# A causal attention layer: ScalarE's copy of the weighed sums, one block of keys earlier in its queue

## The chip, the cores and the metric

The kernel runs on one core of a Trainium2 chip. The metric is the time of one execution on the device, in microseconds (us), as the median of several runs.

## The reference, cut to what matters

The program is a stack of eight layers on x of 4 x 1024 x 128, each added to its input: a state space layer, an expert layer, a landmark attention, an expert layer, a causal attention, an expert layer, an attention with memory, an expert layer. Only the causal attention (16 heads of 8 dimensions, 1024 positions, 4 batches) is touched:

```python
q = q * cos + rotate_half(q) * sin
k = k * cos + rotate_half(k) * sin
bias = rel_bias_table[bucket].transpose(2, 0, 1)
att = (jnp.einsum('bhid,bhjd->bhij', q, k) + bias[None]) * (1.0 / math.sqrt(D))
att = jnp.where(causal[None, None], att, -jnp.inf)
att = jax.nn.softmax(att, axis=-1)
y = jnp.einsum('bhij,bhjd->bhid', att, v)
return y.transpose(0, 2, 1, 3).reshape(B, T, C) @ Wp + bp
```

## The kernel before

`causal_layer` works through 16 units: u = 4 * batch + group, a group being G4 = 4 of the 16 heads. In a unit the queries come in two sets of 512 (q4 = 0 and 1), and each set meets tiles of 128 keys (kt): 4 tiles for the first set, 8 for the second, so `blocks` lists 12 pairs (q4, kt), bi = 0 to 11. Blocks 0 and 4 are the first of a new set of queries.

For each block and head j, TensorE multiplies keys by queries into one of three PSUM banks (4 to 6, `tile_bank`; line 1603). Where keys and queries lie near each other a bias is added, for even j by three matmuls on TensorE (line 1607), for odd j by VectorE (line 1742). ScalarE takes the exponential into `pt` (line 1503). TensorE multiplies the values by `pt` and gathers the weighed sums of the four heads over the key tiles in bank 7 (`products`, line 1625). When a set of queries is through, ScalarE copies bank 7 into `ysb` (`copy_y`, line 1511), and the next set may then overwrite it: the first products of a set (kt == 0) wait for the semaphore `y_copied`, the copy waits for `pv_done`, which counts products. TensorE later transposes `ysb` (`gather_y`, line 1632), and VectorE divides by the sum of weights.

Between the scores TensorE makes, for the next unit, products of queries and keys (`top`, line 1581), of which VectorE takes maxima (lines 1728 and 1729). These, and the projections (line 1545), transposes and outputs of other batches, take turns in two slots of banks 0 to 3; `claim` waits until VectorE or ScalarE has emptied a slot. Projections stand in blocks 4 and 6 of the first two units of a batch, for the batch after it; the values' product (line 1559, moved out by ScalarE at line 1486) stands in block 0 of the third.

The order of all this is written out by hand in `walk`. Each engine runs `walk` with its own functions, and leaves out the steps it has none for, so `walk` is the order of each queue. In an iteration (u, bi) it gives: the scores of heads 0 and 1, a maximum's product, the scores of heads 2 and 3, another, then `products`, then `copy_y` where it is due, then the rest. `products(u, bi)` is always one block behind: it works on block bi - 1, and for bi = 0 on block 11 of the unit before. On ScalarE `scores` are the exponentials. So on ScalarE `copy_y(u, bi)` stands behind the four exponentials of block bi, and on TensorE `products(u, bi)` behind the four scores of block bi.

Of the kernel before, what the change touches and what calls it, by code (L numbers as in the profile page):

```python
# [1183 lines left out]
def causal_layer(nc, g, wq, bq, wk, bk, wv, bv, wp, bp, table, wq_sw, bq_sw, wk_sw, bk_sw, rope, onehot):  # L1184
# [8 lines left out]
    G4 = 4  # L1193
    NG = H // G4
    U = BATCH * NG
# [4 lines left out]
    blocks = [(q4, kt) for q4 in range(2) for kt in range(4 * q4 + 4)]  # L1200
    NB = len(blocks)
    NS = NB * G4
# [14 lines left out]
    def walk(turn_x=idle, project=idle, split=idle, values=idle, turn_bias=idle, stack=idle, top=idle, join=idle, lower=idle,  # L1217
             scores=idle, products=idle, copy_y=idle, gather_y=idle, turn_y=idle, out=idle):
        n = 1
        turn_x(0, n)  # L1220
        n += 1
        for side in range(2):
            for h in range(2):
                project(0, side, h, n)
                n += 1
            for part in range(4):
                split(0, side, part)
        for u in range(3):
            stack(u)
        values(0, n)  # L1230
        n += 1
        for gr in range(NG):
            turn_bias(gr, n)
            n += 1

        def maxima(v, first, count):
            nonlocal n
            u, vb = v // NB + 1, v % NB
            base = sum(QUOTA[(i - LAG) % NB] for i in range(vb))
            for t in range(base + first, base + first + count):  # L1240
                if u < U:
                    top(u, t, n)
                    n += 1
                if u < U and t == ROWS - 1:
                    join(u)

        for t in range(ROWS):
            top(0, t, n)
            n += 1
        join(0)  # L1250
        lower(0, n)
        n += 1
        for v in range(LAG):
            maxima(v, 0, QUOTA[(v - LAG) % NB])
        for u in range(U):
            b, gr = u // NG, u % NG
            for bi in range(NB):
                v = u * NB + bi + LAG
                if bi == 0 and 1 <= u < U - 2:
                    stack(u + 2)  # L1260
                scores(u, bi, 0)
                maxima(v, 0, 1)
                scores(u, bi, 2)
                maxima(v, 1, 1)
                if u or bi:
                    products(u, bi)
                if blocks[bi][1] == 1 and (u or bi > 1):
                    copy_y(u, bi)
                if bi == NB - LAG and u + 1 < U:
                    lower(u + 1, n)  # L1270
                    n += 1
                maxima(v, 2, QUOTA[bi] - 2)
                if bi == 2 and u:
                    gather_y(u - 1, n)
                    n += 1
                if bi == 3 and gr == 0 and b:
                    turn_y(b - 1, n)
                    n += 1
                if bi == 5 and gr == 0 and b:
                    out(b - 1, n)  # L1280
                    n += 1
                if b + 1 < BATCH:
                    if gr == 0 and bi == 1:
                        turn_x(b + 1, n)
                        n += 1
                    for side in range(2):
                        if gr == side and bi in (4, 6):
                            project(b + 1, side, bi // 2 - 2, n)
                            n += 1
                        if gr == side and bi in (7, 8, 9, 10):  # L1290
                            split(b + 1, side, bi - 7)
                    if gr == 2 and bi == 0:
                        values(b + 1, n)
                        n += 1
        products(U, 0)
        copy_y(U, 1)
        gather_y(U - 1, n)
        turn_y(BATCH - 1, n + 1)
        out(BATCH - 1, n + 2)

    with ExitStack() as ctx:
# [53 lines left out]
        st_ready, bias_added, p_ready, pv_done = (s.sem(n) for n in ("st_ready", "bias_added", "p_ready", "pv_done"))  # L1355
        y_copied, yy_ready, oT_ready, x_added = (s.sem(n) for n in ("y_copied", "yy_ready", "oT_ready", "x_added"))

        def slot(n):
            return ps[:, 2 * (n % 2):2 * (n % 2) + 2, :]

        def slot_row(n):
            return slot(n).rearrange("p a b -> p (a b)")
# [7 lines left out]
        def by_vector(bi, j):  # L1370
            return bi in near and j % 2 == 1
# [4 lines left out]
        with nc.Block() as block:  # L1376
# [77 lines left out]
            @block.scalar  # L1454
            def _(act):
                nc.scalar.activation(norm_std[:], g.MV[:, :, 1], ACT.Sqrt, bias=g.eps[:, 0:1]).then_inc(std_ready, 1)

                def turn_bias(gr, n):
                    heads = slice(gr * G4 // 2, gr * G4 // 2 + G4 // 2)
                    turned = slot_row(n).rearrange("p (h r w) -> p r h w", r=2, w=W2)  # L1460
                    act.wait_ge(slot_filled, n + 1)
                    nc.scalar.activation(bias_kp[:, 0, heads], turned[:, 0], ACT.Copy).then_inc(bias_copied, 1)
                    nc.scalar.activation(bias_kd[:, heads], turned[:, 1], ACT.Copy).then_inc(bias_copied, 1)
                    act.wait_ge(bias_rest1, gr + 1)
                    nc.scalar.activation(bias_kp[:, 1, heads], bias_rest[:, gr], ACT.Copy).then_inc(bias2, 1)

                def turn_x(b, n):
                    act.wait_ge(slot_filled, n + 1)
                    nc.scalar.activation(xt[:], slot_row(n), ACT.Copy).then_inc(xt_ready, 1)
                    act.wait_ge(xt_ready, b + 1)  # L1470
                    act.sem_inc(slot_free[n % 2], 1)

                def split(b, side, part):
                    k = b * 2 + side
                    if part == 0:
                        act.wait_ge(full_ready, k * 2 + 2)
                        if k:
                            act.wait_ge(pieces_stored[1 - side], (k + 1) // 2 * NP * 16)
                        nc.scalar.activation(piece[:, 0, :], full[:], ACT.Copy).then_inc(piece1, 1)
                    if part == 2:  # L1480
                        act.wait_ge(rest1, k + 1)
                        nc.scalar.activation(piece[:, 1, :], full[:], ACT.Copy).then_inc(piece2, 1)

                def values(b, n):
                    act.wait_ge(slot_filled, n + 1)
                    nc.scalar.activation(vp[:, b % 2, :, :, 0:D], slot(n).rearrange("p a (t h d) -> p (a t) h d", t=CT, d=D), ACT.Copy).then_inc(vp_ready, 1)
                    act.wait_ge(vp_ready, b + 1)
                    act.sem_inc(slot_free[n % 2], 1)

                def scores(u, bi, j0):  # L1490
                    lo, mid, hi = span(*blocks[bi])
                    c0 = blocks[bi][0] * CHUNK
                    for j in range(j0, j0 + 2):
                        i = u * NS + bi * G4 + j
                        if by_vector(bi, j):
                            act.wait_ge(bias_added, added(u, bi, j))
                        else:
                            act.wait_ge(st_ready, i + 1)
                        if i >= 8:
                            act.wait_ge(pv_done, i - 7)  # L1500
                        if i == 0:
                            act.wait_ge(bias_split, NG)
                        nc.scalar.activation(pt[:, i % 8, lo - c0:hi - c0], ps[:, tile_bank(i), lo - c0:hi - c0], ACT.Exp, scale=SCALE).then_inc(p_ready, 1)  # L1503

                def copy_y(u, bi):
                    q4 = 1 if bi == 1 else 0
                    k = 2 * u + (bi > 1) - 1
                    act.wait_ge(pv_done, u * NS + (0 if bi == 1 else 4 * G4))
                    if k >= 2:
                        act.wait_ge(yy_ready, k // 2)  # L1510
                    nc.scalar.activation(ysb[:, k % 2, :], ps[:, 7, :], ACT.Copy).then_inc(y_copied, 1)  # L1511

                def turn_y(b, n):
                    act.wait_ge(slot_filled, n + 1)
                    nc.scalar.activation(oT, slot_row(n), ACT.Copy).then_inc(oT_ready, 1)
                    act.wait_ge(oT_ready, b + 1)
                    act.sem_inc(slot_free[n % 2], 1)

                walk(turn_x=turn_x, split=split, values=values, turn_bias=turn_bias, scores=scores, copy_y=copy_y, turn_y=turn_y)

            @block.tensor
# [882 lines left out]
```

## Time and profile before

| | us |
|---|---|
| median of 3 runs | 2743.92 |
| lowest, highest | 2735.3, 2744.12 |
| profiled execution | 2740.05 |
| its span | 2738.3 |
| TensorE busy, matmuls | 2201.8 (80%) |
| VectorE busy | 1766.9 (65%) |
| ScalarE busy | 1464.6 (53%) |
| causal layer, about | 850 to 1634 of the span |

The span runs from the first to the last instruction of the profiled execution. In the rows PE is TensorE's matmuls and PEld its weight loads, which overlap them; DVE is VectorE, ACT ScalarE, POOL GpSimd. An fp32 product is recorded as two matmuls, so four heads' products are "x8". The time in brackets at a row's end is how long the engine had been idle before it, with the instruction whose end released it.

### The profile page before, as it was taken

What the parts mean: (1) busy time and instruction counts of PE and PEld (TensorE: products, weight loads), DVE (VectorE), ACT (ScalarE), POOL (GpSimd) and SP (SyncE); (2) the same over time, 40 slices, a digit from 0 to 9 for tenths busy, and PEclk for the clock granted to TensorE, in tenths of its full rate; (3) what the DMA queues carried; (4) which work ended last, traced back from release to release, by engine and by line L of the source; (5) the groups of instructions that cost most, each with busy time, mean ns of one, the idle gap of its engine ahead of it and who ended that gap; (6) DMA issues with size and microseconds to landing.
All of it is one profiled execution on the core that took longest, in us unless ns stands there. A gap on an engine that the chain in (4) does not pass through costs nothing. (4 is left out here: it accounts for less than half of the span.)

```text
span 2738.3 us, 79111 instructions
## 1 busy us (share of the span) xinstructions
PE 2201.8 (80%) x30448; PEld 1559.9 (57%) x30448; DVE 1766.9 (65%) x5714; ACT 1464.6 (53%) x3712; POOL 1058.0 (39%) x1032
## 2 busy tenths in 40 slices
PE   6499948599946888888888877948989898889686
PEld 3188835288832333333333335836777777777486
DVE  6723348623347776776867734359999999999622
ACT  5455544355532455454554545537766676666353
POOL 2156644056651101000000003637766676666164
PEclk7599979599976998998989888979999999999798
DMA  4011120011135111110110001121111111111012
GB/s 127 34 41 43 43 76 1 33 41 43 43 107 152 51 32 34 34 44 19 42 36 22 16 6 48 42 84 54 51 50 52 52 50 52 52 50 50 36 41 89
DMA packets 76023, 134.94 MB, mean 49 GB/s; under 512 B 17225, under 2 KB 32264, under 8 KB 73224
## 3 DMA queue, kind: packets, MB, share of 16 engines
q1 hardware_dynamic: 62080, 102.07, 12.1%
q0 software_dynamic: 13568, 27.81, 3.5%
q8 instruction: 250, 4.10, 0.6%
q14 instruction: 117, 0.96, 0.1%
q10 hardware_dynamic: 8, 0.00, 0.0%
HBM read 65.19 MB, written 32.79 MB: 36 GB/s over the span
## 5 line engine op out<-in xcount | busy, mean ns | idle before, releaser
L1503 ACT ACTIVATE ca_pt<-ca_ps 128x512 f32<-128x512 f32 (+3 forms) x768 | 340.8, 491 | 375.1 <-PE ca_ps L1607 171.7
L733 PE MATMUL ffn_ps<-ffn_xst,ffn_up_w 128*128 128x128 f32 x3392 | 421.2, 278 | 0.2 <-issue 0.2
L733 PEld LDWEIGHTS ffn_ps<-ffn_xst,ffn_up_w 128*128 128x128 f32 x3392 | 403.3, 195 | 1.2 <-issue 1.2
L856 DVE TENSOR_TENSOR ffn_hid<-ffn_sg,ffn_ps 128x512 f32<-128x512 f32 x212 | 145.9, 688 | 333.9 <-PE ffn_ps L733 242.8
L580 POOL DMA_INDIRECT ffn_y<-ffn_ys,ffn_result_at x212 | 208.9, 985 | 222.0 <-DVE ffn_ys L862 191.3
L575 POOL DMA_INDIRECT ffn_xs<-ffn_x,ffn_token_at x212 | 205.2, 968 | 230.8 <-DVE ffn_token_at L839 133.4
L1603 PE MATMUL ca_ps<-ca_stacks 75*128 75x512 bf16 (+3 forms) x768 | 252.5, 352 | 18.0 <-ACT ca_pt L1503 12.6
L1728 DVE TENSOR_REDUCE ca_m_far<-ca_ps 128x1 f32<-128x128 f32 (+5 forms) x384 | 236.5, 616 | 46.4 <-PE ca_ps L1581 44.8
L1581 PE MATMUL ca_ps<-ca_stacks 72*128 72x512 bf16 (+3 forms) x768 | 229.1, 365 | 41.3 <-DVE ca_m_near L1729 28.7
L543 POOL MEMSET ffn_gate_wide<- 128x32 f32 x4 | 0.5, 126 | 580.0 <-POOLq L42 580.0
L1936 POOL TENSOR_TENSOR im_pt_e<-im_pt,im_own 128x512 f32<-128x512 f32 x128 | 162.7, 1271 | 156.6 <-DVE im_pt L2195 154.5
L1625 PE MATMUL ca_ps<-ca_pt,ca_vp 128*9 128x512 f32 (+3 forms) x1536 | 181.0, 545 | 42.5 <-ACT ca_ysb L1511 42.5
L1729 DVE CUSTOM_DVE_ANT_0 ca_spill<-ca_ps,ca_bias_q 128x256 f32<-128x256 f32 (+1 forms) x512 | 200.7, 397 | 18.0 <-PE ca_ps L1581 18.0
L642 ACT ACTIVATE ffn_sg<-ffn_ps 128x512 f32<-128x512 f32 x212 | 126.4, 596 | 131.9 <-PE ffn_ps L733 123.9
L1943 POOL TENSOR_TENSOR im_rope_qk<-im_t,im_mates 128x512 f32<-128x512 f32 x128 | 171.9, 1343 | 52.1 <-DMA im_mates<-im_t 49.6
L741 PE MATMUL ffn_ps<-w_w,ffn_hid 128*128 x1136 | 156.1, 280 | 34.6 <-DVE ffn_ys L862 34.5
L1949 POOL TENSOR_TENSOR im_el<-im_ee,im_rr 128x512 f32<-128x512 f32 x128 | 163.3, 1276 | 34.7 <-ACT im_ee L1987 33.4
L1742 DVE TENSOR_TENSOR ca_ps<-ca_ps,ca_bias_kd 128x256 f32<-128x256 f32 (+1 forms) x288 | 109.7, 382 | 94.4 <-PE ca_ps L1603 90.7
L1581 PEld LDWEIGHTS ca_ps<-ca_stacks 72*128 72x128 bf16 x768 | 67.8, 103 | 177.1 <-DVE ca_m_near L1729 98.1
L741 PEld LDWEIGHTS ffn_ps<-w_w,ffn_hid 128*128 128x128 f32 x1136 | 137.8, 191 | 49.1 <-issue 49.1
L862 DVE COPY ffn_ys<-ffn_ps 128x128 f32<-128x128 f32 x212 | 61.8, 292 | 152.4 <-remote 81.0
L1603 PEld LDWEIGHTS ca_ps<-ca_stacks 75*128 75x128 bf16 x768 | 78.2, 102 | 142.0 <-ACT ca_pt L1503 73.2
(336 smaller groups left out, 4926.3 us busy)
## 6 DMA issues: line engine op xcount, KB each, us to landing
im_mates<-im_t SPq DMA_DIRECT2D x256, 128.0 KB
ffn_got<-ffn_y SPq DMA_DIRECT2D x48, 256.0 KB, 5.7
ca_stacks<-scratch_q_piece SPq DMA_DIRECT2D x16, 576.0 KB
ca_stacks<-scratch_k_piece SPq DMA_DIRECT2D x48, 192.0 KB
ffn_x<-ffn_xn SPq DMA_DIRECT2D x32, 256.0 KB, 2.0
w_w<-in_L_ffn_experts_w_dram SPq DMA_DIRECT2D x2, 2048.0 KB, 11.8
ffn_xs<-ffn_x,ffn_token_at POOLq DMA_INDIRECT x212
ffn_y<-ffn_ys,ffn_result_at POOLq DMA_INDIRECT x212
```

The lines of the kernel that those rows point to most:

```text
L575: nc.gpsimd.indirect_dma_start(out=xs[:, n % XS, :], out_offset=None, in_=xn_rows[:, :], in_offset=bass.IndirectOffsetOnAxis(ap=token_at[: ...
L580: nc.gpsimd.indirect_dma_start(out=y_rows[:, :], out_offset=bass.IndirectOffsetOnAxis(ap=result_at[:, n:n + 1], axis=0), in_=ys[:, n % YS, ...
L733: last = nc.tensor.matmul(ps[:, bank, j * P:j * P + P], up_w[:, n % WS, first + j * P:first + j * P + P], xst[:, n % 2, :], start=True, st ...
L741: last = nc.tensor.matmul(ps[:, 5, 0:P], hid[:, n % 2, j * P:j * P + P], down(e, j), start=(j == 0), stop=(j == IB - 1))
L1503: nc.scalar.activation(pt[:, i % 8, lo - c0:hi - c0], ps[:, tile_bank(i), lo - c0:hi - c0], ACT.Exp, scale=SCALE).then_inc(p_ready, 1)
L1581: last = nc.tensor.matmul(slot_row(n)[:, c:e], stacks[0:KD, u % 3, 0, j, qt * P:qt * P + P], stacks[0:KD, u % 3, 1, j, c:e], start=True, s ...
L1603: last = nc.tensor.matmul(ps[:, tile_bank(i), lo - c0:hi - c0], stacks[:, u % 3, 1, j, kt * P:kt * P + P], stacks[:, u % 3, 0, j, lo:hi], ...
L1625: nc.tensor.matmul(ps[32 * j:32 * j + D + 1, 7, lo - c0:hi - c0], vp[:, b % 2, kt, gr * G4 + j, :], pt[:, i % 8, lo - c0:hi - c0], start=( ...
L1728: nc.vector.tensor_reduce(m_far[:, u % 2, t:t + 1], slot_row(n)[:, 0:lo], AX_X, ALU.max)
L1729: nc.vector.tensor_tensor_reduce(spill[:, n % 2, 0:hi - lo], slot_row(n)[:, lo:hi], bias_q[:, h, W2 - (hi - lo):W2], 1.0, NEG, ALU.add, AL ...
L1943: nc.gpsimd.tensor_tensor(rope_qk[:, k % 2].rearrange("p a b -> p (a b)"), t1[:], mates[:, k % 2, :], ALU.subtract).then_inc(S["rope_ready ...
L1949: nc.gpsimd.tensor_tensor(el[:, k % 3].rearrange("p a b -> p (a b)"), ee[:], rr[:], ALU.add).then_inc(S["el_ready"], 1)
```

## The change

`copy_y` moves, in `walk`, from the second block of a new set of queries (kt == 1: bi = 1 and 5) to the first (kt == 0: bi = 0 and 4). The call behind the loop changes only its argument. In the function, the buffer index k and the count of `pv_done` that it waits for are written for the new bi: for bi = 0 still k = 2u - 1 and u * NS, for bi = 4 still k = 2u and u * NS + 16.

```diff
@@ -1264,7 +1264,7 @@
                 if u or bi:
                     products(u, bi)
-                if blocks[bi][1] == 1 and (u or bi > 1):
+                if blocks[bi][1] == 0 and (u or bi):
                     copy_y(u, bi)
@@ -1293,7 +1293,7 @@
         products(U, 0)
-        copy_y(U, 1)
+        copy_y(U, 0)
         gather_y(U - 1, n)
@@ -1503,9 +1503,9 @@
                 def copy_y(u, bi):
-                    q4 = 1 if bi == 1 else 0
-                    k = 2 * u + (bi > 1) - 1
-                    act.wait_ge(pv_done, u * NS + (0 if bi == 1 else 4 * G4))
+
+                    k = 2 * u + (bi > 0) - 1
+                    act.wait_ge(pv_done, u * NS + bi * G4)
                     if k >= 2:
                         act.wait_ge(yy_ready, k // 2)
                     nc.scalar.activation(ysb[:, k % 2, :], ps[:, 7, :], ACT.Copy).then_inc(y_copied, 1)
```

## Rows read from the trace of the kernel before

**Rows 1.** The page: busy us, share of span, instructions, by engine.

```profile
PE 2201.8 (80%) x30448; PEld 1559.9 (57%) x30448; DVE 1766.9 (65%) x5714; ACT 1464.6 (53%) x3712; POOL 1058.0 (39%) x1032
```

**Rows 2.** Busy time in one stretch, the causal layer; PEclk, DMA share, GB/s last.

```profile
850.50:1634.00 783.50, 670.27 (x4296) 275.46 (x4296) 558.87 (x1914) 378.60 (x824) 17.12 (x18) 0.88 0.14 34
```

**Rows 3.** Waits from 885 to 1625: waiting, awaited: total us, times, longest.

```profile
PEld ca_ps L1581 <- DVE ca_m_near L1729: 73.9, 95, 3.9
...
PE ca_ps L1625 <- ACT ca_ysb L1511: 42.5, 31, 1.7
...
ACT ca_ysb L1511 <- PE ca_ps L1625: 0.5, 1, 0.5
```

**Rows 4.** Timeline, start of unit 5: start, us, engine, instruction, idle before.

```profile
1128.60 0.41 PE L1625 MATMUL ca_ps<-ca_pt,ca_vp 128*9 128x128 f32 x8
...
1129.43 0.98 ACT L1503 ACTIVATE ca_pt<-ca_ps 128x512 f32<-128x512 f32 x2 [0.32 <-DVE ca_ps L1742]
...
1130.08 0.34 PE L1603 MATMUL ca_ps<-ca_stacks 75*128 75x384 bf16 x1 [0.25 <-ACT ca_pt L1503]
...
1130.97 1.25 ACT L1503 ACTIVATE ca_pt<-ca_ps 128x384 f32<-128x384 f32 x3 [0.56 <-DVE ca_ps L1742]
...
1132.10 0.62 ACT L1511 ACTIVATE ca_ysb<-ca_ps 128x512 f32<-128x512 f32 x1
...
1132.77 1.05 PE L1625 MATMUL ca_ps<-ca_pt,ca_vp 128*9 128x512 f32 x8 [1.74 <-ACT ca_ysb L1511]
...
1134.40 0.38 ACT L1503 ACTIVATE ca_pt<-ca_ps 128x256 f32<-128x256 f32 x1 [1.68 <-PE ca_ps L1607]
...
1134.51 0.43 DVE L1742 TENSOR_TENSOR ca_ps<-ca_ps,ca_bias_kd 128x256 f32<-128x256 f32 x1 [2.70 <-PE ca_ps L1603]
```

**Rows 5.** Timeline, start of unit 6, with the values' product.

```profile
1177.09 1.03 ACT L1486 ACTIVATE ca_vp<-ca_ps 128x1024 f32<-128x1024 f32 x1 [1.17 <-PE ca_ps L1559]
...
1180.71 1.04 PE L1625 MATMUL ca_ps<-ca_pt,ca_vp 128*9 128x512 f32 x8 [1.43 <-ACT ca_ysb L1511]
```

**Rows 6.** Timeline, blocks 4 and 5 of unit 6, no projection.

```profile
1188.16 2.28 ACT L1503 ACTIVATE ca_pt<-ca_ps 128x512 f32<-128x512 f32 x4 [0.34 <-PE ca_ps L1603]
...
1189.73 0.41 PE L1625 MATMUL ca_ps<-ca_pt,ca_vp 128*9 128x128 f32 x8
...
1191.58 2.06 ACT L1503 ACTIVATE ca_pt<-ca_ps 128x512 f32<-128x512 f32 x4 [1.14 <-PE ca_ps L1603]
...
1194.19 1.90 PE L1625 MATMUL ca_ps<-ca_pt,ca_vp 128*9 128x512 f32 x8 [0.96 <-ACT ca_ysb L1511]
...
1196.87 0.69 DVE L1728 TENSOR_REDUCE ca_m_far<-ca_ps 128x1 f32<-128x512 f32 x1 [2.72 <-PE ca_ps L1581]
```

**Rows 7.** Timeline, block 5 of unit 5, behind a projection.

```profile
1148.56 1.05 PE L1625 MATMUL ca_ps<-ca_pt,ca_vp 128*9 128x512 f32 x8 [0.91 <-ACT ca_ysb L1511]
...
1150.07 0.69 DVE L1728 TENSOR_REDUCE ca_m_far<-ca_ps 128x1 f32<-128x512 f32 x1 [0.60 <-PE ca_ps L1581]
```

**Rows 8.** Timelines of ScalarE and TensorE, unit 15.

```profile
1589.64 4.14 ACT L1503 ACTIVATE ca_pt<-ca_ps 128x512 f32<-128x512 f32 x8 [1.45 <-PE ca_ps L1607]
...
1594.32 1.05 PE L1625 MATMUL ca_ps<-ca_pt,ca_vp 128*9 128x512 f32 x8 [1.53 <-ACT ca_ysb L1511]
...
1605.19 1.71 PE L1625 MATMUL ca_ps<-ca_pt,ca_vp 128*9 128x512 f32 x8 [1.57 <-ACT ca_ysb L1511]
```

**Rows 9.** Products in units 5, 6 and 7, and a stretch of unit 6 (busy time).

```profile
1152.40 1.05 PE L1625 MATMUL ca_ps<-ca_pt,ca_vp 128*9 128x512 f32 x8
...
1197.00:1203.00 6.00, 6.00 (x24) 1.76 (x23) 4.05 (x15) 2.17 (x4) 0.00 (x0) 0.53 0.01 1
...
1200.18 1.90 PE L1625 MATMUL ca_ps<-ca_pt,ca_vp 128*9 128x512 f32 x8
...
1223.35 1.90 PE L1625 MATMUL ca_ps<-ca_pt,ca_vp 128*9 128x512 f32 x8 [1.75 <-ACT ca_ysb L1511]
...
1226.25 0.38 ACT L1503 ACTIVATE ca_pt<-ca_ps 128x256 f32<-128x256 f32 x1 [2.95 <-PE ca_ps L1607]
```

## The prediction

> **What bounds the kernel now.** I read the page's busy shares first [rows 1]: no engine is full, so the answer lies in one layer. The change touches only the causal layer, about 783 us of the span; there TensorE is busy for 670 us, VectorE for 559 and ScalarE for 379 [rows 2]. So TensorE leads, VectorE is close behind, and ScalarE has slack as a whole. What matters is where TensorE stands still. The list of waits over the layer [rows 3] has it: TensorE's largest wait on another engine is at the products of line 1625, for the copy of line 1511: 42.5 us in 31 waits. The next is VectorE's maxima (73.9 us by the weight loads, much of it beside running matmuls). The copy itself waited for TensorE once, for 0.5 us.
>
> I call a set of four heads of one batch a unit; there are 16 (u = 0 to 15), each of 12 blocks, 0 to 3 for the first 512 queries and 4 to 11 for the second. Bank 7 gathers the weighed sums. The last products of an old set of queries are issued on TensorE inside block 0 (or 4) of the new set, the first products of the new one inside block 1 (or 5), and those must not start until the copy has emptied the bank.
>
> A timeline of a unit's start shows why TensorE waits [rows 4]. The last products of the old sum start at 1128.60 and take 0.41. From then on the bank could be copied. But ScalarE's queue has the copy behind the four exponentials of block 1: it starts at 1132.10, and the new products at 1132.77, after 1.74 us of idle TensorE. The copy takes 0.62.
>
> **The change part by part.** Nothing is added or removed: 32 copies stay 32, and the two semaphore counts at each come to the same values. Each copy but the one behind the loop moves up past four exponentials, on ScalarE's queue alone. No DMA and no other queue is touched.
>
> *What the copy waits for in its new place.* At block 0 the old products end at 1129.01, and ScalarE's exponential of the block's last head starts at 1129.43 (first of the pair) and ends about 1129.95. So the sums are ready 0.9 us before ScalarE arrives. At block 4 the products end at 1190.14 and the four exponentials at 1190.44 [rows 6]: a margin of 0.3 us. I cost this wait at nothing; if the margin were gone, ScalarE would have 1.14 us of idle time at that place to cover it. Its other wait, for the gathered sums one unit back, was served two blocks earlier or more.
> The Trainium skill, page "TensorE: Matmul & The Clock Gate", section "Architectural detail: the array is 16× 32×32, not 1× 128×128", says that ScalarE takes its instructions strictly in order; if the copy did wait in its new place, the exponentials of the next block would wait behind it. By that rule alone the gain falls by each microsecond the copy waits beyond its cover; the rows above show none.
>
> *Block 1, ordinary units (u = 1, 3, 4, 5, 7, 8, 9, 11 to 14: eleven).* The stall is 1.74 us each. Here ScalarE is not idle at the new place: the exponential of block 1's first head follows at about 1129.95, and the scores of head 3 need it out of the way (three banks take turns). In the same rows TensorE's scores at 1130.08 had just waited for an exponential already. The moved copy pushes head 0's exponential back by what it adds to ScalarE's queue, 0.55 us (2.06 for four exponentials of 512 is about 0.5 a step, and the copy is as wide [rows 6]). The 0.56 idle in front of 1130.97 takes that up for ScalarE, but head 3's scores come 0.55 later. So TensorE reaches the products 0.55 later and starts them at once: 1.74 - 0.55 = 1.19 each, 11 x 1.19 = 13.1 us.
> *Block 1 of u = 2, 6, 10:* ScalarE next moves the values out (line 1486) and sits idle 1.17 us before it [rows 5]; the copy fits, and the whole 1.43 us goes: 3 x 1.43 = 4.3.
> *Block 1 of u = 15:* ScalarE runs without a gap there; 1.53 - 0.55 = 1.0 [rows 8].
> *Block 5 without a projection (u = 2, 3, 6, 7, 10 to 14: nine).* Between block 4's exponentials and block 5's, ScalarE is idle 1.14 us [rows 6], so the copy costs nothing, and the stall of TensorE goes: 0.96 in the row for u = 6, and over the nine five of 1.29 and one each of 1.19, 1.10, 0.96 and 0.81, together 10.5. What is late next is VectorE, but it was idle for 2.72 us behind this stall, so it is no bound yet. u = 8, where VectorE was also idle for longer than the stall, gives its 0.9.
> *Block 5 with a projection (u = 0, 1, 4, 5, 9: five).* The stall is 0.91, but VectorE, late from the rotary sums, was idle for only 0.60 behind it [rows 7]: it becomes the bound, and 0.6 is what goes: 3.0.
> *Block 5 of u = 15:* 1.57 - 0.55 = 1.0 [rows 8].
> Sum: 13.1 + 4.3 + 1.0 + 10.5 + 0.9 + 3.0 + 1.0 = 33.8 us, out of 42.5. As a check, all the stalls, 25.0 at block 1 and 17.5 at block 5, add up to the 42.5 of the list of waits [rows 3].
>
> *Does it survive downstream?* At 1134.51, behind the stall, VectorE had been idle for 2.70 us and ScalarE's next exponential (1.68 idle) waited for TensorE too [rows 4]. All three start again from TensorE, so an earlier TensorE shifts all of them together; 1.19 is less than 2.70. The loads that could hold the layer back are issued from the same chain and shift as well.
>
> *The clock.* Behind the stall of u = 7 the products take 1.90 us where those of u = 5 take 1.05 [rows 9]: the granted clock is 0.50 there (the lower of the two levels, 1.2 GHz), where the matmuls in front of the stall ran at 1.00. The next exponential comes 2.90 us after the products start, against 1.63 in u = 5, 1.27 more; I read 0.8 to 1.3 at five of the seven units (1, 3, 4, 7, 8, 11, 12) whose first blocks are slow. If shortening the idle time stops these falls, 7 x 1.06 = 7 us come on top; if it only shifts them, none. I take 1 to 2, so a gain of 35.
> The same page of the Trainium skill, section "A second HAM failure mode: psum-queue depth-cycling", says that TensorE's short idle times between groups of matmuls suffice to make its clock go back and forth. This trace agrees in that slow stretches follow such idle times; by the rule the whole 7 us, and some of the next rival's, would be gained.
>
> **The sum.** The profiled execution took 2740.05 us with a span of 2738.3. 2740.05 - 35 = 2705. The median of the three runs is 3.9 above that execution, and would give 2709. I forecast 2707.
>
> **The rivals.**
> *The clock gains a lot.* From about block 5 on, eight units (2, 3, 6, 7, 10, 11, 13, 14) run some 10 us at the low level, TensorE busy 6.00 of 6 us [rows 9]. From block 5's products to block 6's it is 5.99 us there (1194.19 to 1200.18) against 3.84 in u = 5 (1148.56 to 1152.40) with equal work: 2.15 for the first block, about 3.9 for the 1.8 blocks of a slow stretch. Without them up to 31 us more: some 2675, or 2690 for half. Against it: in u = 6 the low level is there from about 1192.5, before the stall began, so idle time that the change leaves alone (VectorE's maxima in blocks 3 and 4) starts it. Chance 0.13.
> *Half is given back.* TensorE arrives earlier at the next claims of a bank for the maxima, where it already waits for VectorE [rows 3]; each block-1 gain then loses the part by which VectorE has no more slack, or the copy stretches the exponentials' chain by more than 0.55. Gain 12 to 26 instead of 35, about 2721. Chance 0.2.
> *It does nothing to be seen.* The wait for the copy turns into one of the same length for head 3's exponential, with VectorE as the next bound at block 5; 2735 to 2748. Against it stand the 0.9 us by which the sums are ready and ScalarE's idle 1.14. Chance 0.07.
> *Slower.* One mechanism: the changed timing lets the clock fall in block 5 also in the units that now keep it. A fall costs 3.9 us, the gain is 34; it takes nine more falls, while eight units are left, so the copy's 0.55 would also have to cost more than it saves at block 1. With all eight and half of the stalls' gain it would be 2740 - 17 + 31 = 2754. Chance 0.05.
>
> **How the numbers follow.** The forecast's own case (gain 28 to 42, 2698 to 2714) has the remaining 0.55. A range of 2690 to 2728 holds it, most of the case of half given back and a part of the clock's; left out are the strongest clock gains, no change, and slower, under 0.2. About 0.3% is what a measurement of this kernel can tell from no change, 8 us. Faster by more: 0.88, within: 0.07, slower: 0.05.
>
> **What would show each step.** TensorE's wait for line 1511 at the products: from 42.5 us to below 3. ScalarE's copy starts about 2 us earlier at a unit's start, right behind the fourth exponential of block 0, and is followed by block 1's first. TensorE's waits for exponentials (line 1503 before 1603) grow by about 11 x 0.55 = 6 us in its own idle time. Waits for VectorE's maxima grow by a few us. The layer's end, before at about 1634, comes 35 us earlier, and what follows it is as long as before. The prediction is wrong if the copy waits for the products, if the layer shortens by less than 26 us, or if the mean clock in the layer (0.88) falls.

## The result, and the profile after

| | before, us | after, us |
|---|---|---|
| median of 4 runs each | 2744.02 | 2663.55 |
| lowest, highest | 2735.3, 2751.01 | 2658.16, 2681.18 |
| profiled execution | 2740.05 | 2658.16 |
| its span | 2738.3 | 2656.4 |

The ratio is 0.974, with a 95% interval of 0.9707 to 0.9773: some 71 us faster by it (62 to 80), while the two medians alone lie 80 us apart. 37 were forecast, and 2690 was the range's low end. In two later comparisons on chips of about the same speed the unchanged changed kernel gave 0.9726 and 0.9713, in a third 0.975.

The page of the changed kernel, busy time by engine, answers [rows 1]: TensorE is busy for 34.8 us less with the same 30448 matmuls, the other engines for the same time. The same matmuls take less time where the clock is at its higher level, as the products' rows further down show (1.05 us for 1.90).

```profile
PE 2167.0 (82%) x30448; PEld 1546.1 (58%) x30448; DVE 1764.9 (66%) x5714; ACT 1463.5 (55%) x3712; POOL 1057.5 (40%) x1032
```

The list of waits of the changed kernel, from 877 to 1552, answers [rows 3]: the 42.5 us are gone. For the copy TensorE waits once, 0.7 us, in the transposes behind the last unit, and the copy for TensorE 0.5 us as before.

```profile
PE ca_ps L1581 <- DVE ca_m_near L1729: 23.2, 42, 3.0
PE ca_ps L1603 <- ACT ca_pt L1503: 16.4, 44, 0.8
...
PE ca_ps L1632 <- ACT ca_ysb L1511: 0.7, 1, 0.7
ACT ca_ysb L1511 <- PE ca_ps L1625: 0.5, 1, 0.5
```

The timeline of the start of unit 5, changed kernel, answers [rows 4]: the copy follows block 0's last exponential, and the products at 1104.00 wait for nothing. (A row at the end of the stretch that was asked for counts only the instructions up to there, here x4 of the eight.)

```profile
1101.27 0.41 PE L1625 MATMUL ca_ps<-ca_pt,ca_vp 128*9 128x128 f32 x8
...
1102.10 0.60 ACT L1503 ACTIVATE ca_pt<-ca_ps 128x512 f32<-128x512 f32 x1 [0.32 <-DVE ca_ps L1742]
1102.59 0.59 ACT L1511 ACTIVATE ca_ysb<-ca_ps 128x512 f32<-128x512 f32 x1
...
1103.07 1.44 ACT L1503 ACTIVATE ca_pt<-ca_ps 128x384 f32<-128x384 f32 x3
...
1103.62 0.34 PE L1603 MATMUL ca_ps<-ca_stacks 75*128 75x384 bf16 x1 [0.20 <-ACT ca_pt L1503]
...
1104.00 0.62 PE L1625 MATMUL ca_ps<-ca_pt,ca_vp 128*9 128x512 f32 x4
```

Where the rest went is seen in the causal layer's loop, from the first exponential to the last unit's transposes: 737.9 us before, 672.4 after. One row of busy times for each, columns as in [rows 2], the granted clock third from the end (before first). TensorE's busy time fell by 29.7 us and its idle time, the rest of the loop, by 35.7 (from 99.1 to 63.4): the first is the clock's part, the second the stalls'.

```profile
885.77:1623.66 737.89, 638.79 (x4203) 264.46 (x4201) 526.26 (x1799) 375.66 (x821) 17.12 (x18) 0.91 0.13 33
```

```profile
878.32:1550.77 672.45, 609.07 (x4203) 253.59 (x4201) 525.67 (x1799) 374.17 (x821) 17.13 (x18) 0.96 0.15 36
```

The loop gives 65.5 us of the 81.9 by which the spans differ. The other 16 lie half in front of the loop and half behind it, in code that the change does not touch: the loop began at 885.8 and 878.3, and 1114.6 and 1105.6 us were left behind it. Most of it lies in the four expert layers, which were 1.6 to 5.1 us shorter each. In the further traces on chips of this speed it began at 873.6 to 886.5, and 1107.5 to 1116.7 us were left, for either order; so I count them to no kernel.

For the clock I use a sum: in windows of 1 us, 2 x (1 - granted clock) is the time in them at the lower level (1.2 GHz, a granted 0.50). I call it **low time**. Over the loop it is 138.9 us before and 57.6 after.

The distance between two units shows both parts. First transposes of the gathered sums in units 1, 2 and 3, TensorE's timeline, before and then after (only the start of each row counts here; each was asked for in a stretch of 1 us, which cuts it):

```profile
944.52 0.66 PE L1632 MATMUL ca_ps<-g_ident,ca_ysb 128*128 128x128 f32 x4
...
992.46 0.77 PE L1632 MATMUL ca_ps<-g_ident,ca_ysb 128*128 128x128 f32 x5
...
1036.52 0.66 PE L1632 MATMUL ca_ps<-g_ident,ca_ysb 128*128 128x128 f32 x4
```

```profile
933.42 0.77 PE L1632 MATMUL ca_ps<-g_ident,ca_ysb 128*128 128x128 f32 x5
...
979.18 0.98 PE L1632 MATMUL ca_ps<-g_ident,ca_ysb 128*128 128x128 f32 x7
...
1015.49 0.77 PE L1632 MATMUL ca_ps<-g_ident,ca_ysb 128*128 128x128 f32 x5
```

From unit 1 to 2 the clock is high throughout in both: 47.94 becomes 45.76, 2.2 us, the stalls alone (0.60 + 1.43 by the prediction). From unit 2 to 3 it is 44.06 and 36.31, 7.75 us: the two stalls explain 2.5 to 3.0, and before there were 13.6 us of low time here, after none. Where the changed kernel still has a long slow stretch, behind block 4 of unit 6 (10.2 us of low time), that distance is 40.44: 4.1 us for the stretch. Its products show the two levels:

```profile
1162.47 1.90 PE L1625 MATMUL ca_ps<-ca_pt,ca_vp 128*9 128x512 f32 x8
1168.46 1.90 PE L1625 MATMUL ca_ps<-ca_pt,ca_vp 128*9 128x512 f32 x8
1173.03 1.05 PE L1625 MATMUL ca_ps<-ca_pt,ca_vp 128*9 128x512 f32 x8
```

### The profile page after: what moved, and what is told of

Its sections match the earlier page's. It is cut to its first block and busy times, and to the rows that moved or that the text cites. A ratio compares the mean times of both kernels' runs of the same rounds, so it can differ in the third digit from the quotient of the medians.

```text
span 2656.4 us, 79111 instructions
## 1 busy us (share of the span) xinstructions
PE 2167.0 (82%) x30448; PEld 1546.1 (58%) x30448; DVE 1764.9 (66%) x5714; ACT 1463.5 (55%) x3712; POOL 1057.5 (40%) x1032
## 5 line engine op out<-in xcount | busy, mean ns | idle before, releaser
L1603 PE MATMUL ca_ps<-ca_stacks 75*128 75x512 bf16 (+3 forms) x768 | 242.2, 338 | 22.2 <-ACT ca_pt L1503 16.4
L1581 PE MATMUL ca_ps<-ca_stacks 72*128 72x512 bf16 (+3 forms) x768 | 221.7, 352 | 43.5 <-DVE ca_m_near L1729 30.8
L1625 PE MATMUL ca_ps<-ca_pt,ca_vp 128*9 128x512 f32 (+3 forms) x1536 | 167.7, 509 | 0.0
L649 ACT ACTIVATE ffn_up_w<-w_w 128x1024 f32 x142 | 150.0, 1057 | 14.9 <-DVE ffn_table_e L828 3.6
```

Of the source, the lines that this page charges most:

```text
L1581: last = nc.tensor.matmul(slot_row(n)[:, c:e], stacks[0:KD, u % 3, 0, j, qt * P:qt * P + P], stacks[0:KD, u % 3, 1, j, c:e], start=True, s ...
L1603: last = nc.tensor.matmul(ps[:, tile_bank(i), lo - c0:hi - c0], stacks[:, u % 3, 1, j, kt * P:kt * P + P], stacks[:, u % 3, 0, j, lo:hi], ...
L1625: nc.tensor.matmul(ps[32 * j:32 * j + D + 1, 7, lo - c0:hi - c0], vp[:, b % 2, kt, gr * G4 + j, :], pt[:, i % 8, lo - c0:hi - c0], start=( ...
```

## The experiments

There were chips of two speeds: in most comparisons the kernel before took 2737 to 2752 us, in two of them 2675 to 2678, with the expert layers shorter. So ratios are compared, and loops, which don't show that difference: the loop of after_filled takes 663.2 us on a chip of the faster kind, and of the slower kind, as after_filled2, 662.5. Line numbers behind an edit move by its length. All traces:

| kernel | ratio to before (95%) | loop, us | low time, us |
|---|---|---|---|
| before | 1 | 737.9 | 138.9 |
| before_again | | 744.7 | 155.8 |
| after | 0.974 (0.9707 to 0.9773) | 672.4 | 57.6 |
| after_again | 0.9726 (0.9688 to 0.9764) | 681.3 | 85.1 |
| after_third | 0.9713 (0.968 to 0.9746) | 670.5 | 57.2 |
| after_fourth | 0.975 (0.9729 to 0.9772) | 670.3 | 53.5 |
| only_block0 | 0.9897 (0.9873 to 0.9921) | 720.5 | 158.3 |
| only_block4 | 0.9819 (0.9793 to 0.9845) | 701.4 | 77.6 |
| before_filled | 0.984 (0.9816 to 0.9865) | 713.1 | 67.9 |
| before_filled_tiny | 1.0003 (0.9983 to 1.0022) | 745.3 | 156.5 |
| after_waits | 0.9942 (0.992 to 0.9964) | 724.2 | 118.8 |
| copy_behind_head0 | 0.9734 (0.9709 to 0.976) | 677.7 | 78.1 |
| after_filled | 0.9728 (0.9704 to 0.9752) | 663.2 | 30.6 |
| after_filled2 | 0.9755 (0.9724 to 0.9786) | 662.5 | 33.9 |
| head0_filled | 0.9743 (0.9718 to 0.9768) | 662.1 | 40.6 |
| after_filled_block4 | 0.9767 (0.9738 to 0.9796) | 672.0 | 47.4 |
| after_filled_tiny | 0.9785 (0.9762 to 0.9808) | 676.6 | 68.3 |
| after_filled_pad2 | 0.9735 (0.97 to 0.9771) | 662.2 | 33.7 |
| after_filled_pad34 | 0.9715 (0.9678 to 0.9753) | 662.4 | 33.8 |
| after_filled_pad66 | 0.9681 (0.9644 to 0.9719) | 662.4 | 33.8 |

**The same kernels again.** Is the low time a property of the order, or luck of one execution?

> The kernel before, unchanged, for a second trace. Theory 1 (the clock): of the 64 us by which the causal layer's loop became shorter (737.8 to 673.6), the idle time at the copies gives 34 to 42 and TensorE's clock the rest; then the low level must last about 130 to 150 us in the layer in every run of this kernel, at places that may move, and the loop take 730 to 745. Rival (an accident of one run): low time here under 110 us, loop under 725. Outside the loop, where the code is the same, both traces should differ by no more than some 10 us.

> The changed kernel, unchanged, for a second trace and times. Theory 1: low level 50 to 90 us in the layer, loop 665 to 690, time 2655 to 2685. Rival (the low time of 66 us was luck of that run): low time over 110 and time near 2700, the 34 to 42 us of the stalls alone.

Measured: 155.8 and 85.1 us; with after_third and after_fourth the changed order has 53.5 to 85.1, the old one 138.9 to 155.8. The order sets it. Between traces of one order the loop changes by 6.8 us for 16.9 of low time (0.40), and by 11.0 for 31.6 (0.35, after_again against after_fourth). With 0.37 the 81.3 us of low time between the first two traces are worth 30 us, and of 65.5 there are 35 left for the stalls, as the busy and idle times said.

**One of the two places at a time.**

Against the changed kernel, only_block0 and only_block4 (in `copy_y` the count waited for follows, in only_block4 the buffer index too):

```diff
-                if blocks[bi][1] == 0 and (u or bi):
+                if (bi == 0 and u) or bi == 5:
```

```diff
-                if blocks[bi][1] == 0 and (u or bi):
+                if (bi == 1 and u) or bi == 4:
```

> Only the copy at a unit's start is moved up (block 1 to block 0); the one for the second queries stays at block 5. Stalls of TensorE for the copy: 17.5 us stay, 25 go. By stalls alone the gain is 18 to 25 us, about 2722. Theory 1: with the 7 short slow stretches at the units' starts gone and the slow stretches at block 5 still there, 7 us more: 2712 to 2718, low time 110 to 130. Rival (the two places help one another: a slow stretch needs both stalls close together): low time under 90 and about 2695.

> Only the copy between the two sets of queries is moved up (block 5 to block 4). Stalls for the copy: 25 us stay, 17.5 go. By stalls alone the gain is 15 to 17 us, about 2728. Theory 1: the long slow stretches begin at block 5, so most of the clock's gain comes with this one: low time 70 to 100, 2695 to 2708. Rival (the long slow stretches come from VectorE's maxima in blocks 3 and 4, not from the stall): low time stays above 120 and the time is about 2728.

Each list of waits has just the stalls of the place that was left; only_block0 first, then only_block4:

```profile
PE ca_ps L1625 <- ACT ca_ysb L1511: 17.5, 16, 1.6
```

```profile
PE ca_ps L1625 <- ACT ca_ysb L1511: 25.0, 15, 1.7
```

only_block4 came out as the clock's theory had it: with fewer microseconds of stall removed it gains more (1.8% against 1.0%), since its low time is halved. It is faster than expected: 2688.1 us for 2695 to 2708, though that chip ran the kernel before at 2736.7 and 0.9819 of 2744 would be 2694. only_block0 missed one half: low time did not fall at all (158.3); slow stretches of 7 to 10 us stand at block 5 of nearly every unit. The seven short ones at units' starts did go, but units 1, 5 and 9, which in the trace of before keep the high level there, now have 6.8, 6.8 and 10.2 us of low time. Its loop can be set beside before_again and before_filled_tiny, which have the same low time: 720.5 against 744.7 and 745.3, so moving the copy at block 1 gives 24 to 25 us (18.4 were forecast). Measured at the place itself, from the start of the old products to the start of the new ones, the fifteen unit starts get shorter by 21.6 us against before_again; where the other 3 come from is not shown. The removal of these stalls brought nothing from the clock by itself.

**Idle time filled, nothing moved.** This is the run that tells the clock from the order: TensorE gets work in the stall, and the products behind it start no earlier (64.6 us from old products to new ones over the fifteen unit starts, 64.9 before).

```diff
                     if kt == 0 and (u or q4):
+                        nxt = u * NS + (bi + 2) * G4
+                        pe.wait_ge(p_ready, nxt - NSB + 1)
+                        for _ in range(4 if q4 else 5):
+                            nc.tensor.matmul(ps[:, tile_bank(nxt), :], ident_bf[:], bias_kp[:, 0, 0:2, :].rearrange("p h w -> p (h w)"),
+                                             start=True, stop=True, skip_group_check=True)
                         pe.wait_ge(y_copied, 2 * u + q4)
```

> The order of before, with 5 (block 1) or 4 (block 5) matmuls of 128x512 added in front of the wait for the copy. They write a bank that the next scores overwrite, cost about 0.22 us each at the high clock and lie in TensorE's idle time of 0.8 to 1.75 us, so every new set's first products still wait for the copy. Theory 1 (the idle time at the copies makes the clock fall, and that cost 25 to 30 us beside the stalls): low time in the layer falls from about 140 to 155 us to under 100, and the time falls by 12 to 30 us against before, to 2707 to 2725, with no stall removed. Rival (the clock falls for other reasons; the gain came from the order alone): low time stays above 130, time 2735 to 2760, since what sticks out of the idle time is added.

> As before_filled, with the same number of added matmuls at the same places behind the same wait, but of 4 columns instead of 512: the instructions are there, TensorE is hardly any busier. Theory 1 (it is TensorE's idle time that lets the clock fall): nothing is gained, ratio 0.997 to 1.003, low time 130 to 160 us. Rival (the added wait or the instructions themselves changed the order of something): a ratio near the 0.984 of before_filled.

The old order with useless matmuls in its idle time is 1.6% faster (some 40 us, more than the 12 to 30 expected), with low time 67.9. The same instructions with 4 columns for 512 change nothing: 1.0003, low time 156.5. The loops, before_filled and then before_filled_tiny (the clock third from the end):

```profile
833.07:1546.20 713.13, 638.61 (x4311) 268.64 (x4340) 525.21 (x1799) 376.04 (x821) 17.17 (x18) 0.95 0.14 34
```

```profile
885.50:1630.80 745.30, 651.38 (x4342) 271.69 (x4340) 526.57 (x1799) 375.99 (x821) 17.16 (x18) 0.89 0.13 33
```

32 us between them for 88.6 of low time: 0.36, the same price again. The profiled execution of before_filled was the slowest of its six, 14 us above their median, which is one reason why the whole times show more than the loops. (Of the 139 wide matmuls the trace holds 108, so TensorE's busy times are not to be compared.) That TensorE's idle time at the copies costs it its clock is shown, not only argued. Which of its matmuls' properties the chip looks at is not.

**The stall put back into the new order.**

```diff
                         pe.wait_ge(y_copied, 2 * u + q4)
+                        pe.wait_ge(p_ready, u * NS + (bi + 2) * G4)
```

> The changed kernel with TensorE's stall put back: the first products of a new set wait for all four exponentials of the block in front, as they did in effect before, while ScalarE copies early. The copy's own 0.6 us is no longer in the stall, but the exponentials are 0.3 us later at block 1. Theory 1: stalls of some 30 us return, low time goes back above 110 us, the time is 2705 to 2730, most of the gain gone. Rival (the early copy helps in another way, by freeing the copy's buffers or ScalarE's time): low time under 90, below 2695.

The early copy stays and the stall returns. The list of waits has 24.9 us of it, which it puts down to "issue", since it names no releaser for this second wait:

```profile
PE ca_ps L1626 <- issue: 24.9, 30, 1.1
```

With the stall come low time (118.8) and nearly all of the time (0.9942). At 0.37 per microsecond of low time the loop of after (672.4, 57.6) would be 695 at 118.8; 724.2 is 29 more, about the stalls. For the rival, some other use of the early copy, at most the 0.6% is left.

**The copy one exponential later.**

```diff
                         nc.scalar.activation(pt[:, i % 8, lo - c0:hi - c0], ps[:, tile_bank(i), lo - c0:hi - c0], ACT.Exp, scale=SCALE).then_inc(p_ready, 1)
+                        if u and bi == 1 and j == 0:
+                            copy_y(u, 0)
```

(and no copy at bi == 0 in `walk`)

> The changed kernel, but at a unit's start the copy stands behind the first head's exponential of block 1 instead of in front of it. In the changed kernel the scores of block 1's head 3 came 0.36 us later than before, relative to the old products, since that exponential waits behind the copy. If that displacement is on the path, 11 to 12 units give 0.3 each: 3 to 4 us, 2655 to 2664. Rival: the copy then ends too late for the first products, and the stall returns in part: 5 us slower, near 2670.

0.9734 beside 0.9713 to 0.975 for the changed kernel: no difference that these runs can tell. By distances between units there is one: 36.00 for the changed kernel's 36.27 to 36.31 where the clock is high, 0.3 each, as expected. Some 3 us are below what the times resolve.

**The idle time that is left.** TensorE also idles for VectorE's maxima in blocks 3 and 4; this fills it in the changed kernel, behind the products:

```diff
+                    if bi == 2 or bi == 3 and (gr >= 2 or b == BATCH - 1):
+                        nxt = u * NS + (bi + 2) * G4
+                        pe.wait_ge(p_ready, nxt - NSB + 1)
+                        for _ in range(bi):
+                            nc.tensor.matmul(ps[:, tile_bank(nxt), :], ident_bf[:], bias_kp[:, 0, 0:2, :].rearrange("p h w -> p (h w)"),
+                                             start=True, stop=True, skip_group_check=True)
```

> The changed kernel with matmuls of 128x512 added in TensorE's idle time in front of VectorE's maxima: 2 behind the products issued in block 3, 3 behind those in block 4 where no projection follows. If idle time in blocks 3 and 4 starts the slow stretches that are left (low time 58 and 85 us in two traces, all long ones starting 1 to 3 us behind block 4's copy), they go: low time under 40 us, 8 to 15 us faster, 2650 to 2658. Rival (the filling lies on the path, 0.22 us each, 60 or so of them, 13 us, or delays VectorE's work): 2665 to 2678 with low time unchanged.

> after_filled unchanged, on the same chip as after_third. Its loop was 663 us with 31 us at the low level, 9 to 18 us shorter than the two traces of the changed kernel, while the median did not show it. If the loop's gain is real: ratio 0.966 to 0.970, 8 to 15 us below after_third. If it is an accident of that trace: same as after_third within 5 us.

> Both: the copy behind the first head's exponential of block 1, and the filling in blocks 3 and 4. If the copy's displacement of head 3's scores is on the path, 3 to 4 us below after_filled2, about 655 to 660 us for the loop with low time under 40; ratio 0.964 to 0.969. If not, the same as after_filled2.

Low time fell to 31 to 41 us and the loop to 662 to 663, 7 to 8 below the best trace of the changed order, while the same matmuls with 4 columns (after_filled_tiny) leave 68.3 and 676.6: the theory holds there too. head0_filled came out like after_filled2, so the copy's new place still shows nothing. But the time did not follow: on one chip after_third gave 2672.29 and after_filled2 2681.31, where 8 to 15 us less had been expected. What ate it lies 190 us later, in the memory attention layer, whose code is the same. Its busy times from first to last, after_third and then after_filled2:

```profile
1745.40:2482.10 736.70, 640.65 (x19779) 538.33 (x19784) 665.34 (x2022) 490.82 (x1665) 496.06 (x391) 0.98 0.15 52
```

```profile
1734.80:2492.90 758.10, 653.79 (x19784) 546.94 (x19784) 672.12 (x2022) 490.94 (x1665) 494.57 (x391) 0.96 0.15 51
```

> The changed kernel unchanged, on the chip of the two below: ratio 0.970 to 0.977; memory attention layer 735 to 741 us as in all traces but those of after_filled, after_filled2 and head0_filled.

> after_filled with added matmuls of 4 columns instead of 512. The filled kernels had a causal loop 8 to 18 us shorter, but their memory attention layer, which is the same code and comes some 190 us later, took 755 to 761 us instead of 735 to 741. If that comes from the added instructions themselves (62 more in TensorE's stream, which moves all later code), it stays: memory layer 755 or more and the loop like the changed kernel's, ratio near 0.980. If it comes from TensorE's work or from the time at which the layer starts: memory layer 735 to 741, ratio 0.970 to 0.977, low time 55 to 90 us.

> Filling only behind block 4's products, 3 matmuls of 512 columns in the ten units without a projection. If idle time in block 4 is what starts the long slow stretches that are left: low time 30 to 50 us and a loop of 662 to 668. If block 3's idle time matters as much: low time 55 or more. If the longer memory layer comes from the number of added instructions, it is here 735 to 741 or another length than with 62; ratio 0.966 to 0.972 if it is not longer.

after_fourth had 733.9 us there, after_filled_tiny 754.4, after_filled_block4 756.2. So it isn't the added work: 62 matmuls of 4 columns do it, and 30 wide ones (after_filled_block4). Nor is it the clock alone: over that layer it is 0.98 in after_filled_tiny, as in after_fourth. Filling block 4 alone brought low time to 47.4, within the first expectation's 30 to 50, but its loop of 672.0 is not shorter; by this one trace block 3's idle time seems to matter too.

Then the number of added instructions, by matmuls of 4 columns behind the layer's last output:

```diff
+                pe.wait_ge(p_ready, U * NS)
+                for _ in range(66):
+                    nc.tensor.matmul(ps[:, 4, 0:4], ident_bf[:], bias_kp[:, 0, 0, 0:4], start=True, stop=True, skip_group_check=True)
```

> after_filled with 2 matmuls of 4 columns behind the causal layer's last output on TensorE, so 64 added matmuls in all. They take no time to speak of. If the memory layer's length depends on where its instructions lie in the stream, it comes out differently for 62, 64, 96 and 128 added matmuls, at 735 to 741 us for some; with the filled loop of some 663 us the ratio is then 0.965 to 0.970. If every added stream lengthens it: 754 to 761, ratio 0.973 to 0.978.

> As after_filled_pad2 with 34, 96 added matmuls in all; the same two expectations.

> As after_filled_pad2 with 66, 128 added matmuls in all; the same two expectations. before_filled, with 139 added, had a memory layer of 745 us and before_filled_tiny 737.

With 62, 64, 96 and 128 added the memory layer takes 754 to 761, 747.1, 747.4 and 732.9 us, beside loops that agree within some 1 us, after_filled_tiny's apart. before_filled and before_filled_tiny, both with 139 added at other places, had 744.6 and 737.0. That layer in after_filled_pad66:

```profile
1672.50:2405.40 732.90, 640.99 (x19778) 538.95 (x19784) 662.23 (x2022) 490.81 (x1665) 495.97 (x391) 0.98 0.15 53
```

So its length goes with the instructions that TensorE's stream has in front of it, by up to 28 us. The number is not all, since 139 gave two lengths. How it works, the runs don't show; it is left open. after_filled_pad66 is the best kernel of the study, 0.9681, with an interval (0.9644 to 0.9719) just below that of after_fourth and overlapping those of the other runs of the changed kernel. It was not run beside the changed kernel on one chip, so that it beats it is likely and not settled.

## Why the prediction was wrong, point by point

**The stall and its cause** were right: the 42.5 us were ScalarE's queue, and all of them went. In unit 5 the copy starts 1.32 us behind the start of the old products, for 3.50 before.

**The copy's own wait** was costed at nothing, and it is nothing: 0.5 us in one place, before and after. The rule of the Trainium skill on ScalarE's strict order ("TensorE: Matmul & The Clock Gate", "Architectural detail: the array is 16× 32×32, not 1× 128×128") took nothing away here: these 0.5 us are the only wait of a copy in the list.

**Block 1** was sized too small. Between the old products and the new ones it is 4.17 us before (1128.60 to 1132.77, [rows 4]) and 2.73 after (1101.27 to 1104.00): 1.44, not 1.19. The scores of head 3 are 0.36 us later relative to the old products, not 0.55. Over all fifteen unit starts these distances shorten by 21.8 us (64.9 to 43.1), and only_block0 gives 24 to 25 us at equal low time, for 18.4 predicted.

**Block 5** can't be read as well, since the clock changes with it. What is left of 35 us after block 1's 22 to 24 is 11 to 13. only_block4 against before_again gives 43.3 us for 78.2 of low time, at 0.37 another 14 for the stalls; 15.4 were predicted. All stalls together: 33.8 predicted, about 35 measured.

**Downstream** little was given back: TensorE's wait for VectorE's maxima rose from 21.2 to 23.2 us, for exponentials from 12.6 to 16.4 (6 were expected on top).

**The clock is the step that failed.** "I take 1 to 2" stood where 30 belonged. The prediction had the price of a slow stretch right: 3.9 us for a long one, 4.1 measured. It had the rival too, up to 31 us more and 2675, at a chance of 0.13; that is the case that came, and 0.974 of 2744 is 2673. (That the median lies 11 us lower still belongs to the 16 us outside the loop, which no step of the prediction covers and I count to no kernel.) What misled was one argument: in unit 6 the level was low 0.8 us before the stall began (1192.4 and 1193.2), so idle time that the change leaves alone was said to start the stretches. That much was right: idle time in blocks 3 and 4 takes part, as after_filled shows, and in the changed kernel the clock still falls within 1.5 us of the same place in units 6, 7, 10, 11, 13 and 14. What was wrong is that the change would therefore leave the stretches as they are: it made them short. Stretches of 10 us or more: eight before, eight in before_again, one in after, three in after_again, none in only_block4 and before_filled, while 10 of the 12 that after has left last 3.4 us. Low time went from 138.9 to 57.6. I also priced only the falls at units' starts, whose stalls only_block0 removed without any fall in low time, and left the long ones, by far the larger sum, at nothing.
The Trainium skill's section "A second HAM failure mode: psum-queue depth-cycling" of the same page names this mechanism, short idle times of TensorE that make its clock go back and forth. The runs agree with it, with 156.5 us of low time with narrow matmuls and 67.9 with wide ones; it gives no size, but weighed by it the rival deserved far more than 0.13.

**The range** ended at 2690, above the full clock gain, which was left out as part of two in ten.

## What to carry to other kernels

When a TensorE-bound stretch holds both stalls and slow matmuls, price a removed stall twice: its own length, and a share of the low time around it (here 0.37 us for each microsecond at the low level, and 81 us of those hung on 42.5 us of stall). Ask not only what starts a slow stretch but what keeps it long: idle time that the change removes can lengthen one that other idle time began. The first reading afterwards is TensorE's busy and idle time over the same loop: with the same instructions, less busy time is the clock's part and less idle time the stalls'. A cheap test before any reordering: fill the stall with useless wide matmuls and leave the wait where it is; what that gains is the clock's part. Compare loops and stages, not only whole times, since code far behind an edit can get longer with the instruction stream in front of it.

## What the runs showed of the hardware that I had not expected

- Useless work made a kernel faster: 139 matmuls of 128x512 in TensorE's idle time took 1.6% off, the same number with 4 columns nothing (0.984 and 1.0003).
- Removing the larger sum of stalls (25.0 us at block 1) changed low time not at all; removing the smaller (17.5 at block 5) took it from 139 to 156 down to 77.6. Here, where the idle time lies counts for more than how much it is.
- The same code of the memory layer took 732.9 to 760.9 us, and only kernels with instructions added in front of it in TensorE's stream were above 741.
